# Winograd products in an attention kernel: the second product of each set is accumulated onto the first one's PSUM bank, and ScalarE copies the sum out in place of VectorE's addition

## What is computed

```
q  = einsum("bsd,de->bse", h, wq)         # 32 heads, 128 columns of each are used
kv = einsum("bsd,de->bse", h, wkv)        # k and v of 32 heads, 128 columns each
scores = where(causal, q k^T * 192**-0.5, -1e30)   # within a batch of 32 tokens
attn   = softmax(scores) v
x      = x + attn @ wo
```

## Time and profile before

| engine | busy us | share of the span |
|---|---|---|
| TensorE, matmuls | 2087.6 | 99% |
| VectorE | 1369.5 | 65% |
| GpSimd | 1260.0 | 59% |
| ScalarE | 718.9 | 34% |

### The profile page before, as it was taken

How to read it: one execution, slowest core, us unless ns; L and a number is a source line. 1 busy time by engine, 2 the same in 40 slices (tenths; PEclk the granted TensorE clock), 3 DMA queues, 4 the chain that set the end, 5 groups by cost and what they waited for, 6 DMA issues and landing times. The chain is left out here.

```text
span 2118.0 us, 36935 instructions
## 1 busy us (share of the span) xinstructions
PE 2087.6 (99%) x11914; PEld 1810.2 (85%) x11914; DVE 1369.5 (65%) x2615; ACT 718.9 (34%) x1444; POOL 1260.0 (59%) x1319
## 2 busy tenths in 40 slices
PE   7999999999999999999999999999999999999999
PEld 5888888989898898989888898989887778878887
DVE  8767677676777676665656566565656776645444
ACT  5333232332323232332323233222323744443332
POOL 4578585767767576776758576776746642133220
PEclk9999999999999999999999999999999999999999
DMA  7421212211111226111111211111112200001110
GB/s 242 155 63 46 55 50 79 54 52 47 50 52 45 80 59 220 52 41 41 40 40 43 66 50 40 40 40 40 40 62 74 96 21 0 0 1 40 40 40 20
DMA packets 123783, 122.43 MB, mean 58 GB/s; under 512 B 35905, under 2 KB 102113, under 8 KB 121793
## 3 DMA queue, kind: packets, MB, share of 16 engines
q1 hardware_dynamic: 92865, 110.01, 16.8%
q10 hardware_dynamic: 29568, 7.34, 1.6%
q0 software_dynamic: 1280, 4.20, 0.7%
HBM read 108.27 MB, written 13.28 MB: 57 GB/s over the span
## 5 line engine op out<-in xcount | busy, mean ns | idle before, releaser
L217 PE MATMUL psum<-yc,wh 128*128 128x512 f32 x904 | 360.9, 399 | 0.3 <-PEq L270 0.3
L219 PE MATMUL psum<-yc,wh 128*128 128x512 f32 x904 | 352.6, 390 | 0.0
L218 PE MATMUL psum<-yc,wh 128*128 128x512 f32 x904 | 352.1, 389 | 0.0
L1478 DVE TENSOR_TENSOR resid<-psum,resid 128x512 f32<-128x512 f32 x248 | 171.2, 691 | 138.7 <-PE psum L219 134.4
L217 PE MATMUL psum<-kept,yc 128*128 128x256 f32 x896 | 253.6, 283 | 1.6 <-DVE u L1427 0.9
L1023 POOL TENSOR_TENSOR wh<-wh_f,wh 128x256 fp32r<-128x256 f32 x256 | 189.3, 749 | 106.4 <-ACT wh L989 104.4
L219 PE MATMUL psum<-kept,yc 128*128 128x256 f32 x896 | 250.8, 280 | 0.0
L218 PE MATMUL psum<-kept,yc 128*128 128x256 f32 x896 | 250.4, 280 | 0.0
L219 PEld LDWEIGHTS psum<-yc,wh 128*128 128x128 f32 x904 | 169.6, 188 | 36.3
L1023 POOL TENSOR_TENSOR wh<-raw,wh 128x256 fp32r<-128x256 f32 x192 | 142.2, 741 | 92.5 <-ACT wh L989 92.5
L217 PEld LDWEIGHTS psum<-yc,wh 128*128 128x128 f32 x904 | 170.1, 188 | 31.5 <-issue 0.7
(11 more groups left out here) (367 smaller groups left out, 4899.7 us busy)
## 6 DMA issues: line engine op xcount, KB each, us to landing
raw<-in_attn_w SPq DMA_DIRECT2D x96, 512.0 KB, 5.1
wo_f<-in_attn_w SPq DMA_DIRECT2D x31, 512.0 KB, 4.0
hankel<-kernel_rows SPq DMA_DIRECT2D x32, 256.0 KB, 4.8
y_parts<-stage ACTq DMA_DIRECT2D x56, 128.0 KB, 2.3
yc<-y_parts SPq DMA_DIRECT2D x7, 1024.0 KB, 5.3
resid<-in_xT SPq DMA_DIRECT2D x4, 1024.0 KB, 9.7
outT<-wide SPq DMA_DIRECT2D x16, 256.0 KB, 2.6
kept_f<-in_l_w SPq DMA_DIRECT2D x3, 1024.0 KB, 5.6
```

Of the source, the lines that this page charges most:

```text
L217: pe.matmul(out, w[0], x[0], start=start, stop=False)
L218: pe.matmul(out, w[0], x[1], start=False, stop=False)
L219: return pe.matmul(out, w[1], x[0], start=False, stop=stop)
L1478: dve.tensor_tensor(part, psum[:, 5 + (GH + m) % 3, :], part, ALU.add).then_inc(tail_free, 1)
```

## The change

`product_bank` is written more shortly; it gives the same banks. P6 no longer starts a new sum in its bank but is accumulated onto P1 (`onto`), so that the bank holds P1 + P6. For that the first P6 moves to bank 6, where the first P1 lies, and waits for P1's copy too. ScalarE copies the bank to `u2` (`keep_u2`, new), right before `keep_p5` of each set (in set 0 the store of a part lies between). VectorE's addition k = 0 is gone. In its place VectorE waits for ScalarE's copy and then counts `mix_done` on, so that all waits on that count stay as they were. `p1_done` now counts two copies per set. In P1 of a v set only the first of the bank's two halves starts a sum anew.

```diff
-        def mm3(pe, out, w, x, start, stop):
+        def mm3(pe, out, w, x, start, stop, onto=False):
-            pe.matmul(out, w[0], x[0], start=start, stop=False)
+            pe.matmul(out, w[0], x[0], start=start, stop=False, skip_group_check=onto)
...
 def product_bank(s, j):
-    return (s * 7 + (-3, 0, 1, 2, 3, 5, 6)[j]) % 3
+    return (s + (0, 0, 1, 2, 0, 2, 0)[j]) % 3
...
+            def keep_u2(it, s, bank=None):
+                g = it * SETS + s
+                act.wait_ge(prod_done, product_count(g, 1))
+                act.wait_ge(mix_done, g * 5 + 5)
+                act.activation(u2[:], psum[:, product_bank(s, 1) if bank is None else bank, :], ACT.Copy).then_inc(p1_done, 1)
...
                 hw.high(act, it, "H1", (0,))
+                keep_u2(it, 0, FIRST_BANK if first else None)
                 store(0)
                 keep_p5(it, 0, first)
...
                 hw.high(act, it, "V", (0,), fresh=first)
+                keep_u2(it, 1)
                 keep_p5(it, 1)
...
             def mix(it, s, k):
                 g = it * SETS + s
                 j = (1, 3, 4, 5, 6)[k]
+                if k == 0:
+                    dve.wait_ge(p1_done, g * 2 + 2)
+                    dve.sem_inc(mix_done, 1)
+                    return
                 dve.wait_ge(prod_done, product_count(g, j))
-                out, other = ((u2[:], p1), (destination(s, 0, 0), p1), (u3[:], u2[:]),
+                out, other = (None, (destination(s, 0, 0), p1), (u3[:], u2[:]),
                               (destination(s, 1, 0), u3[:]), (destination(s, 0, 1), u2[:]))[k]
-                if k == 0:
-                    dve.wait_ge(p1_done, g + 1)
-                    dve.wait_ge(mix_done, g * 5 + 5)
...
-                bank = FIRST_BANK if start else product_bank(s, j)
+                onto = name == "P6"
+                bank = FIRST_BANK if start or (fresh == 0 and s == 0 and onto) else product_bank(s, j)
...
-                if name == "P6":
-                    if not (fresh == 0 and s == 0):
-                        pe.wait_ge(p1_done, g + 1)
+                if onto:
+                    pe.wait_ge(p1_done, g * 2 + 1)
...
                             mm = mm3(pe, out, (yc[:, j, 0, c, at], yc[:, j, 1, c, at]), (w[0][:, n], w[1][:, n]),
-                                     c == 0, c == 1)
+                                     c == 0 and not onto and not (name == "P1" and i), c == 1, onto or name == "P1")
```

More of the change, by code:

```diff
@@ L213, in const @@
             return consts[:, a:b]
-        def mm3(pe, out, w, x, start, stop):
-            pe.matmul(out, w[0], x[0], start=start, stop=False)
-            pe.matmul(out, w[0], x[1], start=False, stop=False)
-            return pe.matmul(out, w[1], x[0], start=False, stop=stop)
+        def mm3(pe, out, w, x, start, stop, onto=False):
+            pe.matmul(out, w[0], x[0], start=start, stop=False, skip_group_check=onto)
+            pe.matmul(out, w[0], x[1], start=False, stop=False, skip_group_check=onto)
+            return pe.matmul(out, w[1], x[0], start=False, stop=stop, skip_group_check=onto)
         later = {
@@ L1329, in body @@
                 hw.high(act, it, "H2", (0,))
+                keep_u2(it, 2)
                 keep_p5(it, 2)
@@ L1335, in body @@
                 store(4)
+                keep_u2(it, 3)
                 keep_p5(it, 3)
@@ L1342, in body @@
                 hw.high(act, it, "H3", (0,))
+                keep_u2(it, 4)
                 keep_p5(it, 4)
@@ L1354, in body @@
                     hw.high(act, it + 1, "H0", (0,))
+                keep_u2(it, 5)
                 keep_p5(it, 5)
@@ L1715, in product @@
                         mm = mm3(pe, psum[:, bank, :], (w[0][:, n], w[1][:, n]), (yc[:, j, 0, c, :], yc[:, j, 1, c, :]),
-                                 c == 0, c == 1)
+                                 c == 0 and not onto, c == 1, onto)
                 mm.then_inc(prod_done, 1)
```

## The result

| kernel | runs | median us | range us |
|---|---|---|---|
| before | 10 | 2121.72 | 2120.84 to 2122.90 |
| changed | 10 | 2127.1 | 2125.92 to 2128.57 |

The ratio is 1.0025, with a 95% interval from 1.0017 to 1.0034: 5.4 us slower, where 6.2 were forecast. The profiled execution took 2127.27 us, span 2125.5. In code, L1277 is now ScalarE's copy of `u2`, L1271 that of P1, L1431 VectorE's wait for the copy, L1440 its additions, L1458, L1463 and L1464 the softmax shift (scaling, maximum, subtraction), L1485 `o_low`, L1738 `scores`.

A forecast was written before the change was run, and what follows sets the result against it. TensorE, 99% busy and without waits in bodies 1 to 15, was taken as the bound. Body 0 with the start, 2.4 us, plus set 1, 3.8 us, made 6.2 us: median 2121.46 to 2127.7 us, range 2122.3 to 2132.0.

The forecast's parts named there:

- the sign: Whole kernel: slower, median from 2121.46 to 2127.7 us, 0.29% more; slower was given a chance of 0.59.
- the two places: Set 1 of bodies 1 to 15, costing 3.8 us, and body 0 with its start, costing 2.4 us.
- the mechanism: Where ScalarE is busy at P6's end, its copy is late; VectorE and its queue stand at the new wait.
- Nothing won back: Bodies 1 to 15: the 66 us of additions taken off VectorE return nothing; no gain counted for GpSimd.
- Start, 0.9 us: First P6 now waits for P1's copy and starts at about 91.05 in place of 90.19, 0.9 us late.
- Body 0, 2.4 us with the start: Sets 2 and 3 of body 0: late copies delay P7 of set 3 by 2.4 us, the start's 0.9 included.
- P7's cover, 2.6 us: Before P7, 24 matmuls 0.11 us apart give the copy 2.6 us, enough in all sets of bodies 1 to 15.
- Set 1, the chain: Bodies 1 to 15: late copy delays the shift; subtraction ends 1.22 us later, `o_low` at 948.19 in place of 946.97.
- Set 1, the last link: First weight load of `output(T, 0)`: 0.29 us late in 12 looped bodies, 0.10 in bodies 7, 8, 15; 3.8 us.

The follow-up runs named there:

- the last two experiments: Full change, VectorE's wait behind set 1's shift and body 0 set 2's transposes: 2123.61 us; the same with body 0's set 0 as before the change: 2122.64 us.

## Why the prediction was right, and where not

It named the sign, the two places and the mechanism, and the time lies 0.6 us under the forecast. That closeness is in part luck: 1.1 us too much for set 1 stand against 0.35 us in body 1 that it didn't foresee. By its own steps:

- **Nothing won back.** Held: the variant with 90 copies and no harmful wait is the same as before. VectorE's busy time fell by 60 us in the full change where 66 were counted, and GpSimd's stayed as it was (1259.6 us, 1260.0 before), as counted.
- **Start, 0.9 us.** Held: 92.25 - 1.11 = 91.14 where 91.05 was worked out.
- **Body 0, 2.4 us with the start.** Held, link by link. On the clock of before: transposes 120.56 (predicted 120.5), k = 1 at 122.38 (122.3), k = 2 at 125.70 (125.9), GpSimd's block 126.54 (126.65), P7 of set 3 at 133.83 (133.8). Total 2.45.
- **P7's cover, 2.6 us: misread.** The 0.11 us between 948.14 and 948.25 lie between a weight load and its matmul, not between two matmuls. Matmuls of 256 columns start 0.12 us apart (107.09 and 107.21 in the kernel before), so the 24 take 2.8 us. The conclusion stands, since bodies 1 to 15 have no wait at P7.
- **Set 1, the chain.** Held. From P6's end (944.70; 939.32 before) the copy ends after 3.12 us (predicted 3.23), the shift starts after 3.42 (3.3 to 3.6), the subtraction ends after 6.62 (6.62) and `o_low` after 8.88 (8.87). The Trainium skill, "SBUF — State Buffer", section "Who interferes with whom", says that a VectorE instruction with two SBUF inputs contends with GpSimd's reads; the runs with repeated maxima show it, with the size of GpSimd's instruction as the step, and the first to start is served first there. The words "whoever issues first", which the prediction draws on, stand in that section for VectorE's two-port modes, which it says `tensor_tensor` doesn't have; for the subtraction it is the start 0.07 us ahead in body 15 that bears them out.
- **Set 1, the last link: the term that was mis-sized.** I added 0.19 us for TensorE's register step in the loop, taken from VectorE's row, and 0.05 for the release. The load came 0.13 us after `o_low` in the looped bodies and 0.07 in the written-out ones, so TensorE's step is 0.06 us. The load is then late by 9.01 - 8.82 = 0.19 us, counted from P6's end (953.71 and 948.14). But a late load isn't a loss of the same size, as I took it to be: before, it stood 0.11 us ahead of its matmul, and now the two start together, so the matmul is late by 0.09 us only. On the other side a restarted row of matmuls loses a little: 954.04 - 953.71 = 0.33 us to the second matmul, where 0.24 is usual (954.28 - 954.04). Together about 0.17 us a body in place of 0.29, and much the same in the written-out bodies 7, 8 and 15 (0.13 to 0.19), where I had 0.10. With 0.28 in body 1 that makes 2.7 us in place of 3.8.
- **Body 1 alone, 0.35 us: not foreseen.** `scores` of set 1 waited there for k = 4 of set 0. Before, it ended 0.38 us ahead of them:

```profile
184.11 0.69 DVE L1427 TENSOR_TENSOR qk<-psum,u 128x512 f32<-128x512 f32 x1 [0.51 <-POOL u L1203]
...
185.18 1.27 PE L1725 MATMUL psum<-qk 128*128 128x128 f32 x10
```

In the changed kernel they start 0.05 us behind its end, 188.91:

```profile
188.22 0.69 DVE L1440 TENSOR_TENSOR qk<-psum,u 128x512 f32<-128x512 f32 x1 [0.32 <-POOL u L1203]
...
188.96 1.27 PE L1738 MATMUL psum<-qk 128*128 128x128 f32 x9
```

The head of that chain is ScalarE's copy of set 0. In the changed kernel, and then in the variant with all sets but set 1, where body 1 costs nothing, it reads:

```profile
177.98 0.60 ACT L1277 ACTIVATE u<-psum 128x512 f32<-128x512 f32 x1 [2.07 <-PE psum L219]
...
181.73 0.91 DVE L1464 TENSOR_TENSOR sc<-sc,stat 128x256 f32<-128x256 f32 x1
```

```profile
177.70 0.60 ACT L1287 ACTIVATE u<-psum 128x512 f32<-128x512 f32 x1 [1.78 <-PE psum L219]
...
181.61 0.43 DVE L1477 TENSOR_TENSOR sc<-sc,stat 128x256 f32<-128x256 f32 x1
```

The copy starts 0.29 us later after the same product, and the subtraction behind it falls beside GpSimd again and takes 0.91 us for 0.43. The traces of the last two experiments differ in the same way (2.07 with 0.33 us lost in body 1, 1.78 with none). Of all twelve kernels only those with both the late start and the new scheme in set 1 have this loss. Why ScalarE starts later there, in the first pass of the loop, wasn't settled.

## What to carry to other kernels

When work moves from one engine to another, the wait that takes its place is the edit to cost: ask what stands ahead of the new producer in its queue, and what that doesn't need the value stands behind the wait in the consumer's. Here one such wait among 96, put behind the softmax shift that doesn't read the value, took away the whole cost of set 1. On this kernel, whose TensorE has no steady waits, relief of another engine returned nothing, and a hard look at the body that fills the pipeline is worth as much as one at the 15 that follow.

## What the runs showed of the hardware

- Work ahead of a contended instruction can be free or cost a step: VectorE's subtraction, issued beside an instruction of GpSimd, ended 0.28 us behind that one's end. The same 0.33 us ahead of it cost 0.00 the first time and 1.2 us the second, and in the second case a start 0.07 us ahead of GpSimd's made it 0.00 again.
- The wait on a count that is worked out in registers cost about 0.06 us on TensorE in the loops (0.13 us from `o_low`'s end to the load, 0.07 where it is written out), against 0.19 on VectorE.
- A single stall of 2.00 us of TensorE was followed by 3.4 us at the lower clock, worth 1.5 us, in one profile; stalls of 1.93, 1.52 and 1.40 us in other kernels in the same stretch of body 0 were not. What decides between them these runs don't show.
